# Vision tower with a mixture of experts on one core: paired gate rows for the shared blocks, and a down product that waits by banks

## The reference

```python
probs = softmax(x @ router_w)                       # x: 592 x 192, 8 experts
gates, idx = top_k(probs, 2); gates = gates / sum(gates)
g = silu(einsum('bsd,edh->bseh', x, w_gate))        # each expert 192 -> 192
u = einsum('bsd,edh->bseh', x, w_up)
routed = einsum('bse,bsed->bsd', dense_g, einsum('bseh,ehd->bsed', g * u, w_down))
shared = silu(x @ ws_gate) * (x @ ws_up) @ ws_down  # 192 -> 768 -> 192
alpha = sigmoid(x @ sg_w + sg_b)
h = h + alpha * shared + (1 - alpha) * routed
```

## Time and profile before

| what | value |
|---|---|
| time, median of 3 runs | 155.68 us (154.63 to 157.39) |
| time of the profiled execution | 155.41 us |
| its span | 153.5 us |
| TensorE matmuls busy | 134.4 us (88%) |
| VectorE busy | 108.5 us (71%) |
| ScalarE busy | 91.0 us (59%) |
| GpSimd busy | 50.6 us (33%) |
| chain that ended last | TensorE 68%, VectorE 10%, ScalarE 8% |

### The profile page before, as it was taken

The page is one execution under the profiler, slowest core; times in us unless marked ns, Lnnn a source line. Parts: engine busy times, 40 slices in busy tenths (PEclk is TensorE's granted clock), DMA queues, the critical chain, the costliest instruction groups (busy, mean ns, idle before and its releaser), DMA issues.

```text
span 153.5 us, 4141 instructions
## 1 busy us (share of the span) xinstructions
PE 134.4 (88%) x1630; PEld 105.3 (69%) x1630; DVE 108.5 (71%) x280; ACT 91.0 (59%) x219; POOL 50.6 (33%) x63
## 2 busy tenths in 40 slices
PE   0239999999999989995679999998899999999991
PEld 0115887794478878984458868886587778787881
DVE  6389959989896999547475999857947623723753
ACT  0398695975997674683279868555544444444430
POOL 7000000500001432000005324586568386477430
PEclk9999999999999999999999999999999999999999
DMA  4999992780002323004995000485000000000003
GB/s 121 398 337 393 286 301 57 241 320 8 0 0 59 71 71 67 4 0 117 394 395 228 0 4 6 112 317 208 0 0 4 0 2 0 4 0 2 0 4 119
DMA packets 9941, 17.85 MB, mean 116 GB/s; under 512 B 2758, under 2 KB 6162, under 8 KB 9922
## 3 DMA queue, kind: packets, MB, share of 16 engines
q1 hardware_dynamic: 9562, 17.25, 34.0%
q10 hardware_dynamic: 360, 0.34, 0.8%
HBM read 16.63 MB, written 0.96 MB: 115 GB/s over the span
## 4 chain that ended last, share of the span: by engine, by line
PE 68%; DVE 10%; ACT 8%; issue 6%; ACTq 3%; POOL 2%; DVEq 0%; POOLq 0%
PE PS L684 20%; PE PS L714 10%; PE PS L458 4%; PE PS L408 3%; PE PS L495 3%; PE PS L573 3%; PE PS L542 3%; PE PS L431 2%; PE PS L429 2%; PE PS L432 2%; POOL vhl L1061 2%; DVE vhl L1448 2%; PE PS L556 2%; PE PS L395 2%; PE PS L599 2%
## 5 line engine op out<-in xcount | busy, mean ns | idle before, releaser
L1070 POOL TENSOR_TENSOR kq<-vhl,kq 128x296 f16<-128x296 f32 x35 | 28.7, 821 | 43.5 <-ACT kq L987 43.5
L1448 DVE SCALAR_TENSOR_TENSOR vhl<-PS,vhl 128x296 f32<-128x296 f32 x36 | 16.8, 465 | 19.9 <-POOL vhl L1061 10.5
L980 ACT ACTIVATE vhl<-PS 128x296 f32<-128x296 f32 x36 | 14.9, 415 | 24.3 <-PE PS L684 22.9
L987 ACT ACTIVATE kq<-vhl 128x296 f16<-128x296 f32 x36 | 16.0, 446 | 6.6 <-DVE vhl L1448 6.4
L1061 POOL TENSOR_TENSOR vhl<-vhl,xs 128x296 f32<-128x296 f32 x14 | 12.6, 899 | 5.6 <-issue 4.9
L1046 POOL TENSOR_TENSOR piece<-stage,piece 128x768 f16<-128x768 f32 (+1 forms) x3 | 4.6, 1525 | 22.7 <-DVE mx L1315 22.7
L1437 DVE TENSOR_TENSOR vhl<-vhl,xs 64x296 f32<-64x296 f32 (+1 forms) x18 | 10.2, 566 | 2.6 <-ACT vhl L980 2.4
L684 PE MATMUL PS<-XAh,piece 128*128 128x296 f16 x48 | 9.5, 290 | 1.6 <-ACT XAh L865 0.7
L684 PE MATMUL PS<-XAh,slab 128*128 128x296 f16 x48 | 10.0, 291 | 0.9 <-DVE vhl L1448 0.9
L431 PE MATMUL PS<-whl,xhl 128*128 128x193 f16 (+1 forms) x40 | 10.5, 263 | 0.0
L429 PE MATMUL PS<-whl,xhl 128*128 128x193 f16 (+1 forms) x40 | 10.5, 263 | 0.0
(11 more groups left out here) (233 smaller groups left out, 375.9 us busy)
## 6 DMA issues: line engine op xcount, KB each, us to landing
slab<-in_w_inner_dram SPq DMA_DIRECT2D x3, 960.0 KB, 9.5
xs<-gate_rows_dram SPq DMA_DIRECT2D x8, 296.0 KB, 5.7
xs<-in_x_inner_dram SPq DMA_DIRECT2D x3, 592.0 KB, 10.5
stage<-in_f_a_dram SPq DMA_DIRECT2D x2, 768.0 KB, 4.9
stage<-in_f_b_dram SPq DMA_DIRECT2D x2, 768.0 KB, 6.8
stage<-in_f_d_dram SPq DMA_DIRECT2D x2, 576.0 KB, 8.2
xhl<-in_f_a_dram SPq DMA_DIRECT2D x1, 768.0 KB, 9.3
xhl<-in_f_b_dram SPq DMA_DIRECT2D x1, 768.0 KB, 10.6
```

The costliest lines, as they stand in the source:

```text
L980: A(silu[:, i % 2, :], PS[:, 3 + 2 * (i % 2), 0:HALF], ACT.Silu, scale=1.0 / XW).then_inc(S["a_silu"], 1)
L987: A(ah[:, f % ABUF, half * HALF:(half + 1) * HALF], hf[:, i % 3, :], ACT.Copy).then_inc(S["a_ah"], 1)
L1070: G.tensor_tensor(al[:, f % ABUF, cols], hf[:, i % 3, :], ah[:, f % ABUF, cols], ALU.subtract).then_inc(S["g_al"], 1)
L1448: V.scalar_tensor_tensor(out=hf[:, i % 3, :], in0=PS[:, 4 + 2 * (i % 2), 0:HALF], scalar=SH / XW, in1=src[:, i % 2, :], op0=ALU.mult, op1= ...
```

## The change

A second broadcast tile `Gpair` is put in `stage`, free once piece 1 is split. For each pair of experts its partitions 0 to 63 hold the gate row of expert 2k and 64 to 127 that of expert 2k+1, brought by two transfers of 64 partitions (148 KB each, semaphore `d_gp[k]` at 32). SP issues expert 0's broadcast, waits for `a_fw` 12 and `v_fw` 12, and issues the rest. The gate multiply of a shared block becomes one instruction on 128 partitions. Down 6 waits for 2, 4 and 5 sums ahead of tiles 0, 2 and 4. All eight broadcasts to `Gb` stay.

```diff
+        Gpair = stage[:, 0:EXPERTS // 2 * N].rearrange("p (k n) -> p k n", k=EXPERTS // 2)
...
+        d_gp = [sem(f"d_gp{k}") for k in range(EXPERTS // 2)]
...
             sp.wait_ge(d_gt, 16)
-            for e in range(EXPERTS):
+            def gate_of(e):
+
                 sp.dma_start(Gb[:, e, :], gate_rows[e:e + 1, :].to_broadcast([P, N])).then_inc(d_g[e], 16)
 
+            def gate_pair(k):
+
+                for m in (0, 1):
+                    e = 2 * k + m
+                    sp.dma_start(Gpair[64 * m:64 * m + 64, k, :],
+                                 gate_rows[e:e + 1, :].to_broadcast([64, N])).then_inc(d_gp[k], 16)
+
+            gate_of(0)
+            sp.wait_ge(S["a_fw"], 12)
+            sp.wait_ge(S["v_fw"], 12)
+            gate_pair(0)
+            gate_of(1)
+            for k in range(1, EXPERTS // 2):
+                gate_of(2 * k)
+                gate_pair(k)
+                gate_of(2 * k + 1)
...
-                if f == ST:
-                    pe.wait_ge(S["v_acc"], TILES)
                 Dh, Dl = split(f // PT_)[3:]
                 for t in range(TILES):
+                    if f == ST and t % 2 == 0:
+                        pe.wait_ge(S["v_acc"], min(t + 2, TILES))
...
                 if two_experts(f) or f == FT - 1:
-                    dve.wait_ge(d_g[f_expert(f)[0]], 16)
-                    dve.wait_ge(d_g[f_expert(f)[1]], 16)
                     cols = slice(half * HALF, (half + 1) * HALF)
-                    e0, e1 = f_expert(f)
-                    for r0, r1, e in ((0, 64, e0), (64, P, e1)) if e0 != e1 else ((0, P, e0),):
-                        last = V.tensor_tensor(sgate[r0:r1, i % 2, :], silu[r0:r1, i % 2, :],
-                                               Gb[r0:r1, e, cols], ALU.mult)
-                    last.then_inc(S["v_sg"], 1)
+                    pair = f_expert(f)[0] // 2
+                    if two_experts(f):
+                        dve.wait_ge(d_gp[pair], 32)
+                        g = Gpair[:, pair, cols]
+                    else:
+                        dve.wait_ge(d_g[EXPERTS - 1], 16)
+                        g = Gb[:, EXPERTS - 1, cols]
+                    V.tensor_tensor(sgate[:, i % 2, :], silu[:, i % 2, :], g, ALU.mult).then_inc(S["v_sg"], 1)
```

## The result

The changed kernel takes 158.17 us (median of 4 runs, 157.89 to 160.95), the kernel before 155.47 in the same comparison: ratio 1.0186, 95% interval 1.0126 to 1.0246. It is slower, by 2.0 to 3.8 us. The profiled execution took 157.89 with a span of 156.1 (before 155.41 and 153.5). A repeat beside other kernels gave 1.0197 (1.0137 to 1.0256). A ratio leaves out executions that took over 1.5% longer than the fastest of their kernel (in the two of them that were profiled the clock had also fallen, near 72 us), a median doesn't, and where the two differ the text goes by the ratio.

A forecast was written before the change was run, and what follows sets the result against it. TensorE sets the pace, so only its waits, about 2.9 us, can be won. +1.45 for the late pair less 0.40 for the shared blocks gives +1.05 us: 156.46 for the profiled execution, 156.7 as a median, range 154.2 to 158.8.

The forecast's parts named there:

- a landing 4.4 us after the issue: Rival, chance 0.12: pair 0's second half lands at 110.9, delaying product 14 and half block 16; +2.95 us, median 158.6.
- SP's wait: SP's queue after expert 0's broadcast: `v_fw` 12 comes only at 106.1, so the first pair is issued 9.2 us later.
- The landing: Pair 0's arrival ahead of product 14: taken as 109.0, half block 16 at 110.05, down 6 late by 1.45 us.
- the lower bound: Earliest landing of pair 0's second half: issue at 106.15 + 0.35, plus 2.05, so 108.55.
- the stores: Two 192 KB transfers at the kernel's end, landing after 2.0 and 2.1 us, used to estimate pair 0's landing.
- The broadcast row with 3.7: First of the eight present broadcasts, 296 KB, landing 3.7 us after issue; gave the upper landing time of 109.85.
- The clock: Rival, chance 0.04: TensorE's 2.4 us idle before half block 16 brings the lower clock; another 3.75 us, 160.5.
- Down 6's wait: Down 6 starting after two sums instead of five: 0.46 us gain by itself, inside the +1.45 of the late pair.
- the rival of the hidden wait: Chance 0.08: pair 0 is in before product 14, TensorE gets back 1.3 us; 154.1, as a median 154.4.
- The shared blocks: Blocks f = 10 and 13: products end about 0.47 us sooner, removing TensorE's waits; 0.40 us gain taken of 0.44.
- Relief elsewhere: Rival, chance 0.06: without transfers from 101 to 106 the slow GpSimd multiply falls to 0.81; about 156.1 or 155.6.
- No cost of the traffic, expert 1's gates in time: Transfers don't slow the engines; expert 1's broadcast lands at 111.3, just in time for half block 16, at most 0.3 late.

The follow-up runs named there:

- the run with 9: The changed kernel with SP's wait for `v_fw` at 9 in place of 12, nothing else: 154.09 us, ratio 0.9908.
- the runs with and without filler: The changed kernel with 22 unused TensorE matmuls added ahead of half block 16's wait, 157.17 us (1.0103), and without them, 158.17 us (1.0186).
- the run with one wait for all sums: The changed kernel with `v_fw` 9 and down 6 waiting for all five sums at once, as before the change: 153.97 us, ratio 0.9887.
- The first run with moved splits: The changed kernel with `v_fw` 9 and piece 2's low parts behind products 10, 13, 14, 19, 20, 21: median 155.00 us, ratio 0.9891.

## Why the prediction was right, and where it was not

The direction, the range (154.2 to 158.8) and the place were right; the forecast of 156.7 was 1.5 us short. That 158.17 lies inside the range is in part luck: its upper end was set for a landing 4.4 us after the issue, which did not come, while the fall of the clock, which came, had been priced at 160.5, outside it. Step by step:

- *SP's wait* held as worked out: `v_fw` 12 is a low part of piece 2, the wait is 9.2 us long (9.2 forecast), and changing that one number undoes the loss. Shown by the run with 9.
- *The landing* was the term that was too small. "Second issue at 106.15 + 0.35, plus 2.05" was the lower bound, and I took 2.9 us after the release, "nearer to the stores". Measured: 3.5. An issue of 64 partitions took 0.56 (two in 1.12) in place of 0.33, and the second half landed 2.9 us after its issue in place of 2.05. The broadcast row with 3.7 was the nearer one: a load of one row to many partitions, as here. From down 5 to half block 16 it took 110.07 - 105.81 = 4.26 us, by the forecast 110.05 - 106.44 = 3.61: the error cost 0.65 us. That the multiply started at 109.05, as forecast, is chance: this execution was 0.6 ahead at that point.
- *The clock* was the rival given 0.04. It came in both profiled executions of the changed kernel, and the mean clock was below 0.99 in all ten. It cost 1.68 us in the profile, 1.3 by the runs with and without filler. The step that failed is the weighing: "against it, that from 70 to 72 TensorE was busy for 0.56 us of 2 and the matmuls after it kept the full rate". That was one execution. The profiled execution of the run with one wait for all sums has the same waits in that place, 1.15 and 0.69 us with 0.56 us of work between, and there the clock falls right behind them. Its busy times by stretches, and its TensorE timeline:

```profile
72.00:73.00 1.00, 0.70 (x3) 0.70 (x4) 0.66 (x3) 0.91 (x6) 0.00 (x0) 0.74 0.83 310
73.00:74.00 1.00, 1.00 (x5) 1.00 (x4) 0.00 (x0) 0.00 (x0) 0.00 (x0) 0.50 1.02 387
```
```profile
72.30 0.87 PE L619 MATMUL PS<-awst,we 128*128 128x192 f32 x2 [0.69 <-ACT we L960]
```

From this row to the first gate/up matmul it takes 4.57 us (76.87 - 72.30), in the profile of before 2.90 (74.98 - 72.08): 1.67 lost, with no difference in the waits ahead of it. The first run with moved splits shows the same fall, at about 72.4 us. So that the clock held near 72 us in the one profile at hand was chance, and no evidence that a wait costs nothing. What decides between the executions is not shown. The price, one half-rate block for 3.75, was too high: the lower level lasted 3.3 us, and about half of that is lost, 1.68.

- *Down 6's wait.* That most of the bankwise gain would be inside the rest was right: alone 0.44 us, with the pair tile in time nothing. In the rival of the hidden wait, though, I had added it to the others as a saving; there the early products had already given it, which the run with one wait shows. The sum of 1.3 for that case, measured 1.4, isn't changed by which part is given the 0.46.
- *The shared blocks.* 0.40 forecast, and the waits of the blocks 8 to 9 and 11 to 12 gave 0.42 (3.76 each now). The later blocks together gave 0.62: block 13 to 14 lost its wait too (4.00 to 3.76), and 9 to 10 took 0.06 more. Block 13 to 14 is a GpSimd block and not the change's by any step of mine. I can't say why; in the trace of before product 31 starts 0.4 us after its GpSimd multiply has ended, others 0.1. VectorE's work fell by 5.4 us and not by 3.8: the forecast took the median of the 16 multiplies of 64 rows, 464 ns, where their mean is 578. No wait hung on this.
- *Relief elsewhere* (0.06) did not come: with no gate transfer between 100 and 105 us the GpSimd multiply at 102.40 still took 1.53 us.
- *No cost of the traffic, expert 1's gates in time:* both held. Expert 1's row landed 4.2 us after its issue at 106.72, so at 110.9, and was wanted at 112.6. (The transfers behind it are twelve and not eleven, which changes nothing.)

By the trace, 1.05 + 0.65 (landing) + 1.68 (clock) - 0.22 (later blocks, 0.62 for 0.40) = 3.16 us, which is +3.78 - 0.62; the medians differ by 2.7, and both lie inside the interval of 2.0 to 3.8.

What stays open: why the clock stayed up in one of four executions with a pause of 1.95 us, what decides near 72 us, and where the 0.25 of block 13 to 14 went.

## What to carry to other kernels

Before a queue waits on a counter, write down which instructions raise it and what each value means: here 12 looks like "two pieces of six", and is nine plus three of another piece. Judge a new wait by two prices, its own length and what the engine at the end of the chain does when it stands still; with TensorE full on either side, an unbroken pause of 2.86 us cost 1.68 us more through the clock. One execution in which a pause did the clock no harm does not show that it never does: look at several, or at their mean clocks. Two edits that remove the same wait are worth one of them.

## What the runs showed of the hardware

A pause of TensorE of 2.86 us was followed by a fall of the granted clock to 0.50, which began about 0.7 us after work had resumed and lasted 3.3 us; after a pause of 1.95 it fell 1.1 us after work had resumed, in the execution that was profiled; after 1.11 (six executions) and 0.83 (the eight that the ratio counts) the mean clocks, 0.997 or more, show no such fall. In a pause of 8.83 us it fell before work had resumed. Waits of 1.15 and 0.69 us with 0.56 us of work between them were followed by a fall in two profiled executions and by none in that of the kernel before. One 296 KB broadcast written as two rows times 64 partitions took 9.4 us to land, where two transfers of one row to 64 partitions took 3.4 together. A GpSimd multiply of 128 x 296 took 1.53 us beside a VectorE split with two inputs from SBUF, and 0.82 at most once no split lay beside it.
